# Last attention group of a decoder layer: a new order on VectorE, and the shared expert's low parts on GpSimd

## The reference

```python
x = x + self_attention_over_the_batch(layernorm(x))
x = x + cross_attention(layernorm(x), ctx)     # 32 query heads, 8 key/value heads of 128, rmsnorm on q and k
x = x + moe(layernorm(x))                      # 16 experts of width 256, top 4, and one shared expert
# the shared expert, t = tokens:
out = out + silu(t @ Sg.T) * (t @ Su.T) @ Sd.T
```

## Time and profile before

| | |
|---|---|
| median of 3 runs | 855.54 us (854.35 to 857.04) |
| the profiled execution | 853.63 us, span 851.8 us |
| mean granted TensorE clock | 0.992 of full speed |
| TensorE matmuls busy | 815.0 us, 96% of the span |
| VectorE, ScalarE, GpSimd busy | 548.3, 508.7, 538.3 us |

### The profile page before, as it was taken

One profiled execution on the slowest core, in us unless ns is written; L12 is line 12 of the kernel. 1 busy time (PEld: TensorE's weight loads), 2 busy tenths in 40 slices (PEclk: granted clock), 3 DMA queues, 4 the chain that ended last, 5 costly groups with the idle time before them and its releaser, 6 DMA issues.

```text
span 851.8 us, 19392 instructions
## 1 busy us (share of the span) xinstructions
PE 815.0 (96%) x6801; PEld 445.4 (52%) x6801; DVE 548.3 (64%) x1021; ACT 508.7 (60%) x1010; POOL 538.3 (63%) x442
## 2 busy tenths in 40 slices
PE   6689999999999999999999999999999999999997
PEld 2664645645645645644644644645455555555553
DVE  6897886587686587686596596897953222222237
ACT  3799986586586586587587586364324444334331
POOL 6953597797697797696797696822334444444431
PEclk9899999999999999999999999999999999999999
DMA  8039436336226326326327324355075576788933
GB/s 323 5 101 270 149 99 224 100 98 224 100 93 222 103 87 230 101 80 218 121 74 238 108 74 149 138 235 174 2 239 173 174 246 224 246 297 279 396 127 148
DMA packets 51739, 142.47 MB, mean 167 GB/s; under 512 B 6368, under 2 KB 8416, under 8 KB 47328
## 3 DMA queue, kind: packets, MB, share of 16 engines
q1 hardware_dynamic: 43568, 116.93, 40.8%
q0 software_dynamic: 7520, 24.65, 8.3%
q10 hardware_dynamic: 592, 0.08, 0.1%
HBM read 97.85 MB, written 41.68 MB: 164 GB/s over the span
## 4 chain that ended last, share of the span: by engine, by line
PE 37%; POOL 26%; issue 15%; DVE 9%; DMA 7%; ACT 3%; SPq 1%; POOLq 0%; DVEq 0%; ACTq 0%
PE ps L1649 8%; POOL ring_mem L618 8%; POOL reg_h L656 7%; DMA stage<-in_wq 5%; PE ps L2080 5%; PE ps L2082 5%; PE ps L2081 5%; POOL reg_h L660 4%; POOL ring_mem L604 4%; POOL ring_mem L611 2%; PE ps L2059 2%; PE ps L2103 2%; PE ps L2105 2%; PE ps L2104 2%; PE ps L2090 1%
## 5 line engine op out<-in xcount | busy, mean ns | idle before, releaser
L1649 PE MATMUL ps<-wo_hi,reg_b 128*128 128x512 f16 x448 | 142.8, 380 | 0.0
L697 POOL DMA_INDIRECT y_rows<-reg_h,to_row x47 | 48.9, 1039 | 112.4 <-ACT reg_h L1090 107.1
L660 POOL TENSOR_TENSOR reg_h<-reg_h 128x512 f16<-128x512 f32 x84 | 114.8, 1367 | 4.7
L656 POOL TENSOR_SCALAR reg_h<-reg_h 128x512 f32<-128x512 f32 x56 | 93.8, 1676 | 33.6 <-ACT reg_h L896 33.5
L1649 PE MATMUL ps<-hT_hi,wq_hi 128*128 128x512 f16 x256 | 97.1, 379 | 1.1 <-DVE ring_mem L1247 0.9
L1649 PE MATMUL ps<-hT_lo,wq_hi 128*128 128x512 f16 x256 | 97.0, 379 | 0.0
L1649 PE MATMUL ps<-hT_hi,wq_lo 128*128 128x512 f16 x256 | 97.0, 379 | 0.0
L618 POOL TENSOR_TENSOR ring_mem<-kv,ring_mem 128x512 f16<-128x512 f32 x64 | 80.3, 1254 | 23.3 <-ACT ring_mem L832 23.3
L1649 PE MATMUL ps<-wo_lo,reg_b 128*128 128x512 f16 x224 | 84.9, 379 | 0.0
L1649 PEld LDWEIGHTS ps<-wo_hi,reg_b 128*128 128x128 f16 x448 | 43.8, 98 | 55.3 <-issue 9.1
L1599 DVE SCALAR_TENSOR_TENSOR reg_h<-ps,reg_h 128x256 f32<-128x256 f32 x47 | 20.0, 425 | 81.2 <-ACT reg_h L1078 78.5
(11 more groups left out here) (329 smaller groups left out, 2052.4 us busy)
## 6 DMA issues: line engine op xcount, KB each, us to landing
ring_mem<-w_split SPq DMA_DIRECT2D x16, 1536.0 KB, 7.5
w_split<-reg_h SPq DMA_DIRECT2D x88, 256.0 KB, 2.1
reg_h<-in_wgu SPq DMA_DIRECT2D x58, 256.0 KB, 3.2
stage<-in_wq SPq DMA_DIRECT2D x8, 1024.0 KB, 8.5
stage<-in_wo SPq DMA_DIRECT2D x8, 1024.0 KB, 5.8
reg_h<-in_wd SPq DMA_DIRECT2D x30, 256.0 KB, 3.1
wkv_st<-in_wkv SPq DMA_DIRECT2D x8, 512.0 KB, 9.2
ring_mem<-in_x_half SPq DMA_DIRECT2D x8, 256.0 KB, 5.5
```

What stands on the lines that cost most here:

```text
L656: pool.tensor_scalar(st, st, WS, None, ALU.mult).then_inc(pre_scaled_pool, 1)
L660: pool.tensor_tensor(hl[:, 1, :], st, hl[:, 0, :], ALU.subtract).then_inc(pre_split, 1)
L697: pool.indirect_dma_start(y_rows, bass.IndirectOffsetOnAxis(ap=to_row[:, r - 1:r], axis=0), y[r % 2], None).then_inc(scattered[r % 2], 16)
L1649: last = pe.matmul(dst, lhsT(c), rhs(c), start=(m == 0), stop=(m == n - 1))
```

## The change

VectorE, last group: `row_max(i, 3)` moves in front of `normalise(i, 1)`; `probs_lo(i, 2)` and `heads_lo(i, 1)`, until now the whole of step t = 0, move in front of `add_output(i - 1, NT - 1)`, `v_lo_part(i, 1, 5)` and `normalise(i, 2)`. The low parts of the shared expert's weights leave VectorE. GpSimd makes them, after the last unit of the routed experts' weights and before the low parts of the tokens. As GpSimd's subtraction doesn't scale, the staged weights are scaled in place first: those of gate and up by ScalarE (`scale_staged`, one more copy per chunk), those of down by GpSimd itself. ScalarE's high parts of the down weights move from t = 4 and 5 to just behind `heads_hi(i, 0)`.

```diff
@@ gpsimd, after iteration(G - 1, True, False) and pre_lo(G - 1, UNITS - 1)
+            def expert_weights_lo(c):
+                pool.wait_ge(weights_scaled, 2 + KC + 1 + c + 1)
+                pool.tensor_tensor(wo_lo[:, c, :], wgu_st[:, c, :], wo_hi[:, c, :], ALU.subtract).then_inc(wgu_split, 1)
+
+            def down_weights_lo(c):
+                pool.wait_ge(wd_hi_done, c + 1)
+                pool.tensor_scalar(wd_st[:, c, :], wd_st[:, c, :], WS, None, ALU.mult).then_inc(wd_scaled, 1)
+                pool.wait_ge(wd_scaled, c + 1)
+                pool.tensor_tensor(wd_lo[:, c, :], wd_st[:, c, :], wd_hi[:, c, :], ALU.subtract).then_inc(wd_split, 1)
+
+            for c in range(KC):
+                expert_weights_lo(c)
+                if c >= KC - IC:
+                    down_weights_lo(c - (KC - IC))
+
             for t in range(NT):
                 pool.wait_ge(h_hi_done, t + 1)
                 pool.tensor_tensor(h_hl[:, t, 1, :], h_tok[:, t, :], h_hl[:, t, 0, :], ALU.subtract).then_inc(h_split, 1)
@@ scalar
             def expert_weights_hi(c):
...
-                act.activation(wo_hi[:, c, :], wgu_st[:, c, :], ACT.Copy, scale=WS).then_inc(wgu_hi_done, 1)
+                act.activation(wo_hi[:, c, :], wgu_st[:, c, :], ACT.Copy, scale=WS)
...
                     if att and not proj and k == 3:
                         heads_hi(i, 0)
+                        down_weights_hi(0)
+                        down_weights_hi(1)
...
                     if not proj and t < KC:
                         expert_weights_hi(t)
-                    if not proj and KC <= t < KC + IC:
-                        down_weights_hi(t - KC)
+                        scale_staged(wgu_st[:, t, :])
@@ vector
                     row_max(i, 2)
                     probs_lo(i, 0)
                     probs_lo(i, 1)
+                    row_max(i, 3)
                     normalise(i, 1)
                     heads_lo(i, 0)
                     add_output(i - 1, NT - 2)
-                    row_max(i, 3)
+                    probs_lo(i, 2)
+                    heads_lo(i, 1)
+                    add_output(i - 1, NT - 1)
                     v_lo_part(i, 1, 5)
-                    add_output(i - 1, NT - 1)
                     normalise(i, 2)
...
-                    if att and t + 2 < NT:
+                    if att and t + 2 < NT and (proj or t):
                         probs_lo(i, t + 2)
-                    if att and t + 1 < NT:
+                    if att and t + 1 < NT and (proj or t):
                         heads_lo(i, t + 1)
...
-                    if not proj and 1 <= t < 1 + KC:
-                        expert_weights_lo(t - 1)
-                    if not proj and 1 + KC <= t < 1 + KC + IC:
-                        down_weights_lo(t - 1 - KC)
```

More of the change, by code:

```diff
@@ L351, in decoder_kernel @@
         gate_split, logits, sig_exp = sem("gate_split"), sem("logits"), sem("sig_exp")
-        wgu_hi_done, wgu_split, wd_hi_done, wd_split = (
-            sem("wgu_hi_done"), sem("wgu_split"), sem("wd_hi_done"), sem("wd_split"))
+        wgu_split, wd_hi_done, wd_scaled, wd_split = (
+            sem("wgu_split"), sem("wd_hi_done"), sem("wd_scaled"), sem("wd_split"))
         gu_ps, silu_done, z32_done, z_hi_done, z_split = (
@@ L1305, in key_lo @@
                 dve.tensor_tensor(k_lo[:, cols], k32[:, th, :], k_hi[:, cols], ALU.subtract).then_inc(k_split, 1)
[L1307 to L1315, removed]
             def pre_lo(q):
```

## The result

The changed kernel takes 860.89 us (median of 8 runs, 858.92 to 864.56), the kernel before, in 8 runs, 856.71 us. The ratio is 1.0051 with a 95% interval of 1.0032 to 1.0070: slower by 0.51%, some 4.4 us (the medians are 4.2 apart), inside the forecast range of 856.4 to 862.3 and 1.6 us over the 859.3 forecast. Of these 1.6 us, 1.2 are the starting point: the forecast added 3.8 us to 855.54, the median of 3 runs, which is 856.71 with 8.

A forecast was written before the change was run, and what follows sets the result against it. It took nearly full TensorE to bound the stage. Token transposes 4.4 us late less 0.54 back made +3.9, taken as +3.8, on the median 855.54: 859.3 us, range 856.4 to 862.3.

The forecast's parts named there:

- The bound: Last attention group: TensorE is nearly full, so relief of VectorE cannot give back more than 2.2 us.
- The fourth maximum: VectorE's earlier row maximum ends GpSimd's 3.14 us wait; last routed-weight unit ends 2.9 us earlier; no TensorE wait removed.
- The order: VectorE's new order removes TensorE's 0.93 us wait at tile 2; a new 1.35 us wait makes tile 3 0.35 late.
- GpSimd's chain: From third chunk to first token low part, 9.8 us back to back; TensorE stands 3.3 us, token transposes 4.4 late.
- Given back: After the first token transposes, the next ones follow by 3.80 us instead of 4.07, twice: 0.54 us back.
- The clock: TensorE's clock after the stand before the token transposes: a fall was left out of the sum, estimated at 1.7 us.
- one of my own signs of being wrong: The forecast is wrong if the clock row shows less than 1.00 after TensorE's stand before the token transposes.
- the main line: Whole kernel: GpSimd's delay of the token transposes costs +3.8 us, 859.3 us, own range 857.3 to 861.6; chance 0.62.
- rival (a): TensorE's clock falls after the new stand before the token transposes, costing 1.7 us; 861.0 to 862.3 us; chance 0.15.
- SP's loads: SP's queue: last store and three ring loads 2.9 us earlier, fourth ring load some 9 us; costed at nothing.
- (b): GpSimd's chain before the first token low part is shorter: +1.0 to +2.4 us, 856.6 to 857.9; chance 0.13.
- (c): GpSimd finishes before the token transposes in time; TensorE's idle 2.18 us goes, 853.3 us; chance 0.10.

The follow-up runs named there:

- best version: Changed kernel with GpSimd's down-weight scalings and subtractions behind the first two chunks, and ScalarE's tile 1 heads high part before its first weight chunk; 854.62 us, ratio 0.9969 to before.
- heads early alone: Changed kernel with only ScalarE's high part of the heads of tile 1 moved ahead of its first weight chunk; ratio 1.0024 to the kernel before.
- pairs last: Changed kernel with GpSimd's two pairs of scaling and subtraction for the down weights moved behind all eight token low parts; ratio 1.0006 to the kernel before.
- doubled scaling: Changed kernel with each GpSimd scaling of the down weights made in two steps, by 8 and by 8; ratio 1.0078 to the kernel before.
- filled stand: Changed kernel with 13 unused matmuls on TensorE in its idle time before the first token transposes; ratio 1.0019 to the kernel before.
- pairs early: Changed kernel with GpSimd's two down-weight pairs of scaling and subtraction behind the first and second chunk's low part; ratio 1.0031 to the kernel before.

## Why the prediction was right, point by point

- **The bound.** TensorE is the limit in this stage and VectorE's relief could give 2.2 us at most. Right: the best version gave 0.66.
- **The fourth maximum.** GpSimd's wait of 3.14 us for it is gone (0.25 left), its queue runs ahead, and TensorE got nothing from it. Right; the last routed-weight unit ends 2.4 us earlier and not 2.9, as its scaling took 1.93 us where it had taken 1.49 (why, see the last section).
- **The order.** The forecast was 0.93 us gained at tile 2 and a wait of 1.35 before tile 3, late by 0.35. Measured: 1.31, late by 0.40. VectorE's idle time for the heads' high part, forecast 1.2, was 1.10, and the run with the heads early alone shows that it is the cause of most of the wait (0.87 of 1.31 us).
- **GpSimd's chain.** Third chunk scaled 12.3 us behind the first heads product by the forecast, 12.26 measured (563.63 + 0.62 less 551.99). The chain was forecast at 9.8 us (its terms add to 9.7) and took 9.35: the two scalings took 1.49 us each, not the 1.93 I chose, and two subtractions 1.53 and 1.36 instead of 1.16. I had read the 1.93 as the price of standing directly behind another instruction; both scalings stand so, and take 1.49. The delay was 3.96 for 4.4, the stand 3.10 for 3.3. That the stand came so near is partly luck: the terms of TensorE's arrival add to 567.5 and not to the 568 that I wrote, so they give a stand of 3.8. The runs with the pairs last and with the doubled scaling show that this chain sets the time.
- **Given back.** 0.54 by the forecast; 0.73 is what remains in the profile, 0.55 of it in the two transposes that the forecast named.
- **The clock.** Here the sum was mis-sized, and one of my own signs of being wrong came: a clock row under 1.00 after the stand. I left the fall of the clock out as a rival with a chance of 0.15, since 3.3 us lay between an idle time that was followed by 1.2 GHz and one that was not the earlier trace rows. It fell, and the filled stand shows its price: 1.57 us, near my 1.7. With it the forecast sum would have been 5.4 on 4.80 in the profile. So what happened was the main line and rival (a) together. The middle of the forecast came near the result by luck, in that terms were off in opposite ways: a delay 0.44 us too long, 0.2 too little given back, and a clock at nothing.
- **SP's loads** earlier by up to 9 us at no cost: the part behind the stage has the same length in both profiles (260.09 and 260.10 us). Right, as far as one profile of each can tell: over all eleven this part lasts between 258.95 and 261.48 us.
- **Rivals (b) and (c).** (b), a shorter chain, happened in part (0.45 us) and was outweighed. (c), GpSimd in time, is what the run with the pairs last does by another order, and its price of 2.18 us doesn't follow: with GpSimd in time the stage is 42.80, as VectorE's order keeps its own stands of 1.31 and 0.59 us.

## What to carry to other kernels

An engine that is idle most of the time can still be just in time for one instruction: look at what its next critical instruction is, and put new work behind that or into the gaps ahead of it, not between. When an order on one engine removes a wait, count what now stands behind the moved instruction before booking the gain; where that engine is full, the wait moves on by one tile. And price a stand of TensorE with its clock too: here the fall cost 1.57 us beside a stand of 3.10.

## What the runs showed of the hardware that was not expected

- The granted clock halved after a stand of only 1.97 us (pairs early: 0.50 over 566 to 568), and after one of 1.21 us behind the routing (pairs last: 0.50 over 606 to 608). It kept 1.00 after one of 2.16 us in an early stage, where the window shown lies inside the idle time; over the 4 us behind it, 58 to 62, it is 1.00 as well. So the length of the last idle time alone does not decide it; what else does stays open here.
- GpSimd's scaling of 128x512 in float32 takes 1.49 us, or 1.93 when a VectorE instruction with both inputs in SBUF runs across its start. The same scaling, at the same place behind the subtraction of the row maximum, before and changed:

```profile
553.95 1.49 POOL L656 TENSOR_SCALAR reg_h<-reg_h 128x512 f32<-128x512 f32 x1
554.92 0.69 DVE L1273 TENSOR_TENSOR ring_mem<-ring_mem,rowinv 128x512 f32<-128x512 f32 x1
```

```profile
553.95 1.93 POOL L656 TENSOR_SCALAR reg_h<-reg_h 128x512 f32<-128x512 f32 x1
553.72 0.81 DVE L1289 TENSOR_TENSOR ring_mem<-ring_mem,rowinv 128x512 f32<-128x512 f32 x1
```

  In the trace of the kernel before, this line makes 56 scalings. The 24 that took over 1.8 us all had such an instruction across their start, the 31 that took 1.51 or less had none; one of 1.56 lies between.
- The other way round, VectorE is held off by GpSimd's subtractions. A VectorE multiply with both inputs in SBUF that starts inside one ends some 0.54 us after it (1.34 and 0.94 us for 0.69, pairs early); 0.55 us into a scaling it takes its 0.69. Where VectorE was first, as in the changed kernel (multiply at 560.13, subtraction at 560.30), the subtraction is the longer one, 1.54 us for 1.16. So work that is moved to GpSimd comes back as time on VectorE, and not only in the run with the pairs last: in the changed kernel three of the eight norms of the token tiles now start inside GpSimd's low part of an earlier tile, and the eight average 0.83 us where they took 0.53. These 2.4 us are over half of what the six moved operations had taken. Here it did no harm: TensorE has no wait behind them in the stage. One of the three, with GpSimd's subtraction beside it at 577.15 to 578.30:

```profile
577.19 1.40 DVE L1341 TENSOR_SCALAR reg_h<-x_res,mv,rstd 128x512 f32<-128x512 f32 x1
```
